# Weighted sums of attention in four groups a step in place of nine

## What is computed

```python
x = L0_attn_x                       # (4, 1024, 256)
xn = _layernorm(x)
x = x + attention(xn) + experts(xn)
# attention: 16 heads of 16 features, scores q k^T, causal mask, a linear bias
#   slope[h] * (j - i), divided by 4, softmax, weighted sum of v, then @ Wo + bo
# experts: 8 experts of 256 hidden features, each token goes to 2 of them;
#   gelu(a) * b, a second product, scaled, summed by the router's weights
```

## Time and profile before

| what | us |
|---|---|
| median of 3 runs | 816.59 (814.65 to 817.5) |
| the profiled execution | 818.57 |
| its span, first to last instruction | 816.8 |
| attention, t = 0 to 4 | 132.82 |
| attention, t = 5 to 12 | 219.84 |
| attention, t = 13 | 25.96 |
| attention, t = 14 and 15 | 47.5 |

### The profile page before, as it was taken

How to read it: one execution, slowest core, us unless ns; L and a number is a source line. 1 busy time by engine, 2 the same in 40 slices (tenths; PEclk the granted TensorE clock), 3 DMA queues, 4 the chain that set the end, 5 groups by cost and what they waited for, 6 DMA issues and landing times.

```text
span 816.8 us, 17685 instructions
## 1 busy us (share of the span) xinstructions
PE 768.0 (94%) x6172; PEld 470.9 (58%) x6172; DVE 545.4 (67%) x1419; ACT 467.1 (57%) x984; POOL 429.9 (53%) x561
## 2 busy tenths in 40 slices
PE   7899999999999999999999999879899999989997
PEld 5555554444444444444444444329788888888876
DVE  5458879999999887888888888303234434334348
ACT  2565557777778677777777777874233323323310
POOL 5765542231324545645475463255586666666676
PEclk9999999999999999999999999999899999999999
DMA  8786562503233135243342350113533333322777
GB/s 199 229 253 218 170 193 74 157 17 106 82 93 85 52 95 132 51 109 100 110 98 71 94 159 16 37 40 97 139 106 108 112 116 102 111 78 87 234 237 243
DMA packets 74912, 98.20 MB, mean 120 GB/s; under 512 B 16588, under 2 KB 54092, under 8 KB 74764
## 3 DMA queue, kind: packets, MB, share of 16 engines
q1 hardware_dynamic: 65960, 78.34, 34.1%
q0 software_dynamic: 8864, 18.72, 7.4%
HBM read 63.53 MB, written 30.75 MB: 115 GB/s over the span
## 4 chain that ended last, share of the span: by engine, by line
PE 55%; issue 10%; POOL 8%; ACT 4%; DVE 4%; DMA 2%; another core or an unknown queue 1%; DVEq 0%; POOLq 0%; ACTq 0%
PE banks L1152 16%; PE banks L753 15%; PE banks L745 13%; PE banks L1337 7%; POOL expert_rows L1241 4%; ACT probs L1090 4%; PE banks L1346 3%; POOL stacks L592 3%; DVE stacks L1436 2%; DMA stacks<-xn_rows,places 2%; PE banks L1267 1%; DVE junk L707 1%; DMA w_gu<-expert_rows 0%; DVE probs L1319 0%
## 5 line engine op out<-in xcount | busy, mean ns | idle before, releaser
L707 DVE CUSTOM_DVE_ANT_0 junk<-banks,mask 128x128 bf16<-128x128 f32 (+7 forms) x512 | 359.3, 752 | 54.9 <-issue 50.8
L1090 ACT ACTIVATE probs<-banks 128x512 f32<-128x512 f32 x576 | 310.9, 607 | 101.2 <-PE banks L753 93.7
L753 PE MATMUL banks<-stacks 105*128 105x512 bf16 (+3 forms) x768 | 198.8, 328 | 10.5 <-issue 7.8
L745 PE MATMUL banks<-stacks 102*128 102x512 bf16 (+3 forms) x768 | 172.6, 326 | 2.7 <-DVE maxima L707 2.4
L883 POOL TENSOR_SCALAR_AFFINE_SELECT probs<-probs 128x512 f32<-128x512 f32 x128 | 79.6, 640 | 102.3 <-ACT probs L1090 98.3
L1319 DVE TENSOR_TENSOR probs<-banks,probs 128x256 f32<-128x256 f32 x71 | 30.0, 422 | 151.5 <-ACT probs L1283 111.9
L753 PEld LDWEIGHTS banks<-stacks 105*128 105x128 bf16 x768 | 65.5, 97 | 103.5 <-ACT probs L1090 38.0
L1152 PE MATMUL banks<-probs,ctxT 128*17 128x256 f32 (+2 forms) x1920 | 114.4, 360 | 2.0 <-DVE banks L1071 1.1
L1241 POOL DMA_INDIRECT expert_rows<-stacks,places x71 | 77.5, 1091 | 67.9 <-ACT stacks L1288 51.7
L745 PEld LDWEIGHTS banks<-stacks 102*128 102x128 bf16 x768 | 69.0, 98 | 73.1 <-DVE maxima L707 18.5
L1283 ACT ACTIVATE probs<-banks 128x256 f32<-128x256 f32 x71 | 27.3, 384 | 111.9 <-PE banks L1337 56.4
(11 more groups left out here) (129 smaller groups left out, 769.6 us busy)
## 6 DMA issues: line engine op xcount, KB each, us to landing
stacks<-qk_parts SPq DMA_DIRECT2D x192, 128.0 KB, 3.1
qk_parts<-ctxT SPq DMA_DIRECT2D x32, 384.0 KB, 3.4
xn_rows<-probs SPq DMA_DIRECT2D x8, 512.0 KB, 5.3
ctxT<-inverse_sums SPq DMA_DIRECT2D x8, 512.0 KB
w_gu<-in_w_gu SPq DMA_DIRECT2D x8, 512.0 KB
stacks<-in_x SPq DMA_DIRECT2D x16, 256.0 KB
ctxT<-expert_rows SPq DMA_DIRECT2D x16, 256.0 KB, 3.1
w_gu<-expert_rows SPq DMA_DIRECT2D x16, 256.0 KB, 5.8
```

The source lines that it names most:

```text
L707: last = dve.tensor_tensor_reduce(junk[:, n % RING, c:c + w], mpsum[:, slot, c:c + w], keep["mask"][:, S - w:S], 1.0, 3 * NEG, ALU.add, AL ...
L745: last = pe.matmul(mpsum[:, slot, at + c:at + e], qs[hq][0:R_MAX, h, qt * P:(qt + 1) * P], ks[hq][0:R_MAX, h, c:e], start=True, stop=True)
L753: last = pe.matmul(score_bank(("S", n, h))[:, c:c + w], ks[hq][:, h, kt * P:(kt + 1) * P], qs[hq][:, h, q0:q0 + w], start=True, stop=True)
L1090: act.activation(probs[:, u % PRING, h], score_bank(("S", n, h)), ACT.Exp, scale=SCALE).then_inc(exp_done, 1)
```

## The change

The weighted sums of steps 0 to 13 are issued in four groups: after p = 4 (5 halves), 9 (5), 13 (4) and 17 (4). So a buffer of probabilities is held longer, and there are four of them in steps 0 to 13; the fourth lies in the last quarter of `w_gu`, so the weights of experts 6 and 7 are loaded in steps 14 and 15 and no longer in steps 11 and 12. Steps 14 and 15 keep the order and the three buffers of before. ACT waits for the last user of its buffer (`PROB_WAS`). Count and sizes of the matmuls, exponentials, maxima and DMAs stay.

```diff
-PRING = 3
+PRING = 4
+PROBS = 3
 SRING = 3
+FEW_FROM = B * NQ - 2
+
+def prob_buffers():
+    buffer, was, last = [], [], {}
+    for n in range(B * NQ * NU):
+        k = n - NU * FEW_FROM
+        buffer.append(n % PRING if k < 0 else (k + 2) % PROBS)
+        was.append(last.get(buffer[n]))
+        last[buffer[n]] = n
+    return buffer, was
+
+PROB_BUF, PROB_WAS = prob_buffers()
...
 PV_AT[4], PV_AT[5], PV_AT[7] = [LOW_LAST], [], [HIGH_FIRST, (3, 0), (3, 1)]
+PV_GROUPED = [[] for _ in range(PAIRS)]
+PV_GROUPED[4] = [(0, 0), (0, 1), (1, 0), (1, 1), LOW_LAST]
+PV_GROUPED[9] = [HIGH_FIRST, (3, 0), (3, 1), (4, 0), (4, 1)]
+PV_GROUPED[13] = [(5, 0), (5, 1), (6, 0), (6, 1)]
+PV_GROUPED[17] = [(7, 0), (7, 1), (8, 0), (8, 1)]
...
-    qs, ks, vals, probs = heads["qs"], heads["ks"], keep["vals"], keep["probs"]
+    qs, ks, vals = heads["qs"], heads["ks"], keep["vals"]
+    probs = [keep["probs"][:, i] for i in range(PROBS)] + [Room(keep["w_gu"][:, 3 * NE * DH // 4:].rearrange("p e h -> p (e h)"))([P, 4, CH])]
...
-            if MAP_FROM <= t < MAP_FROM + NE:
-                e = t - MAP_FROM
+            if t >= FEW_FROM:
+                sp.wait_ge(pv_done, PRING + NU * FEW_FROM)
+            for e in [t - MAP_FROM] if MAP_FROM <= t < MAP_FROM + 3 * NE // 4 else [NE - B * NQ + t] if t >= FEW_FROM else []:
                 sp.dma_start(keep["w_gu"][:, e * DH:(e + 1) * DH], ...
...
-            if h == 0:
-                act.wait_ge(pv_done, n + 1)
-            act.activation(probs[:, u % PRING, h], ...
+            if h == 0 and PROB_WAS[n] is not None:
+                act.wait_ge(pv_done, PRING + PROB_WAS[n] + 1)
+            act.activation(probs[PROB_BUF[n]][:, h], ...
...
-                for u0, half in PV_AT[p] if has(1) else PV_LAST[p]:
+                for u0, half in (PV_GROUPED if t < FEW_FROM else PV_AT if has(1) else PV_LAST)[p]:
...
-        keep["probs"] = sb("probs", [P, PRING, 4, CH])
+        keep["probs"] = sb("probs", [P, PROBS, 4, CH])
```

More of the change, by code:

```diff
@@ L881, in mask_unit @@
             for c in DIAG[u]:
-                part = probs[:, u % PRING, :, c:c + P]
+                part = probs[PROB_BUF[n]][:, :, c:c + P]
                 pool.affine_select(out=part, in_=part, compare_op=ALU.is_ge, fill=0.0, base=0,
@@ L1087, in exp @@
             act.wait_ge(s_ready, m + 1)
-            if h == 0:
-                act.wait_ge(pv_done, n + 1)
-            act.activation(probs[:, u % PRING, h], score_bank(("S", n, h)), ACT.Exp, scale=SCALE).then_inc(exp_done, 1)
+            if h == 0 and PROB_WAS[n] is not None:
+                act.wait_ge(pv_done, PRING + PROB_WAS[n] + 1)
+            act.activation(probs[PROB_BUF[n]][:, h], score_bank(("S", n, h)), ACT.Exp, scale=SCALE).then_inc(exp_done, 1)
         for h in range(4):
@@ L1151, in weighted @@
                 for h in range(4):
-                    last = pe.matmul(cpsum[32 * h:32 * h + VW, q0 % CH:q0 % CH + w], vals[b][:, kt, hq, h], probs[:, u % PRING, h, c:c + w],
+                    last = pe.matmul(cpsum[32 * h:32 * h + VW, q0 % CH:q0 % CH + w], vals[b][:, kt, hq, h], probs[PROB_BUF[n]][:, h, c:c + w],
                                      start=i == 0 and (u, half) in ((0, 0), HIGH_FIRST),
```

## The result

| what | before | after |
|---|---|---|
| median of the runs, us | 817.05 (814.65 to 822.0) | 838.68 (837.11 to 840.26) |
| the profiled execution, us | 818.57 | 838.23 |
| its span | 816.8 | 836.5 |
| attention, t = 0 to 4 | 132.82 | 144.41 |
| attention, t = 5 to 12 | 219.84 | 228.33 |

The four groups make the kernel slower: ratio 1.0263, 95% interval 1.0238 to 1.0288, 21.6 us. All of it lies in the attention. What follows the attention takes 266.6 us, as before (266.7).

A forecast was written before the change was run, and what follows sets the result against it. PE was taken as first by a small margin, with DVE setting the pace after the change; +1.6, +17.1, +4.2 and +5.6 make +28.5 on 818.57, so 847.1 profiled and 845 us median, range 824 to 860.

The forecast's parts named there:

- t = 13, DVE dry in four gaps: Step 13: DVE's work plus four idle gaps make 27.6 us against 25.96, +1.6.
- t = 5 to 12, gaps, router's rest and indirect DMAs: Steps 5 to 12: +4.2 us for gaps and other DVE operations, +5.6 for sums meeting POOL's DMAs (0.7 a step).
- t = 0 to 4, gaps and router: Steps 0 to 4: gaps, plus 11.9 us of router operations outside them, make 149.9 us against 132.82, +17.1.
- t = 14 and 15: Last two attention steps: no term in the sum; moved weight loads expected to be hidden.
- PE's saving: PE, steps 0 to 13: five groups fewer at 0.25 us each save 1.25 us a step, 17.5 if PE alone sets pace.
- waits for slots: PE between groups: the third and later product items wait for DVE to free a slot, giving back the 1.25 us.
- DVE's idle, 0.42k - 0.50: DVE behind each group of k halves: idle 1.21 us for k = 4 and 1.63 for k = 5.
- first by a small margin: Kernel before: PE leads, DVE at most two product items behind; both busy 98% in steps 0 to 4.
- PE sets the pace: Rival, steps 0 to 13: DVE's slots never hold PE, 17.5 us are saved, 799 us; chance 0.08.
- Edits at no cost: Fourth buffer, ACT's waits and later w_gu loads cost nothing; moving loads gains PE and DVE 0 to 0.5 us.
- ACT idle on the sums: Sign at L1152 that the edit fails, ACT waiting for its buffer; that rival: 873 us, chance 0.03.
- ACT catches up before the next group: ACT, needing 20.38 of 25.96 us, idles in a group with three banks but recovers before the next; no cost.

The follow-up runs named there:

- e6: Changed kernel (four groups) with half of the columns of both maxima and exponentials left out; ratio 0.9719 to the kernel before.
- e2: Kernel before (nine groups) with half of the columns of every maximum left out; ratio 0.9871 to the kernel before.
- e3: Changed kernel (four groups) with half of the columns of every maximum left out; ratio 0.9853 to the kernel before.
- e5: Changed kernel with full maxima, but exponentials over half of their columns from the fifth unit on; ratio 1.0277 to the kernel before.
- e7: Changed kernel with seven groups of two or three halves in place of four, fourth buffer kept; ratio 1.0102 to the kernel before.
- e8: Changed kernel with the router's DVE operations put behind the maxima of pairs that end in a group; ratio 1.0285 to the kernel before.
- e11: e1 with one indirect DMA behind each of units 2 to 9, not two behind each of 6 to 9; ratio 0.9897 to the kernel before.
- e1: Changed kernel with the sums back in nine places, fourth buffer and later w_gu loads kept; ratio 0.9971 to the kernel before.
- e12: e6 with one indirect DMA behind each of units 2 to 9 of steps 5 to 12; ratio 0.9664 to the kernel before.
- e9: Kernel before with POOL's indirect DMAs behind units 2 to 5 instead of 6 to 9; ratio 1.0684 to the kernel before.

## Why the prediction was right, point by point

The forecast was 845 us and 28.5 us of loss on the profiled execution; it came to 838.7 and 19.7.

| term | forecast | measured |
|---|---|---|
| t = 13, DVE dry in four gaps | +1.6 | +1.7 |
| t = 5 to 12, gaps, router's rest and indirect DMAs | +9.8 | +8.5 |
| t = 0 to 4, gaps and router | +17.1 | +11.6 |
| t = 14 and 15 | 0 | -2.0 |

- **PE's saving.** 0.25 us a group from the earlier trace rows; e6 against e2 gives 0.27 at most and about 0.16 without the waits for ACT. So that PE gains by fewer groups is shown, its exact price is not. In the changed kernel it is given back in waits for slots, as forecast.
- **DVE's idle, 0.42k - 0.50.** Forecast 1.21 and 1.63, found 1.23, 1.23, 1.66, 1.77. Step 13: 27.6 forecast, 27.62 found. So close a meeting is luck, for cut at DVE's items instead of ACT's copy the same step is 28.01 (26.35 before); the difference of 1.66 us is the same by both cuts. e3 and e5 show that it is DVE: take its work away and the step falls by 1.3 us, take ACT's away and it doesn't fall. The text called PE "first by a small margin" in the kernel before; e2 confirms PE. That DVE's work and idle time, 22.17 and 3.79, add up to the step proves nothing, since they do so whoever sets the pace. What shows how small the margin was is e7: two groups fewer already cost 0.8 us in step 13. From this point on DVE pays more for a merging than PE gains.
- **The rival "PE sets the pace", 799 us.** In the changed kernel it is false. In e6, with both consumers light, PE does set the pace and the saving is real. The Trainium skill, "TensorEngine Tiling (Array Packing)", section Key Properties, says that TensorE drains when the tiling mode changes. The 0.25 us a group of the earlier trace rows agree with it; but the sums differ from the scores in their type too, and no run separates the two. What the saving is worth depends on who must be fed.
- **Steps 0 to 4, the term that was mis-sized.** I let two thirds of 17.8 us of router operations lie outside the gaps, because only three groups end an odd pair. But five steps at 27.62 are 138.1, and the stretch took 144.41: 6.3 us lay outside, a good third. In step 4 the gaps left DVE idle for less than in step 13:

```profile
247.83 1.23 DVE L731 CUSTOM_DVE_ANT_0 junk<-banks,mask 128x1024 bf16<-128x1024 f32 x1 [1.32 <-issue]
...
256.24 1.23 DVE L731 CUSTOM_DVE_ANT_0 junk<-banks,mask 128x1024 bf16<-128x1024 f32 x1 [0.73 <-PE banks L769]
262.36 1.23 DVE L731 CUSTOM_DVE_ANT_0 junk<-banks,mask 128x1024 bf16<-128x1024 f32 x1 [0.30 <-issue]
```

  Gaps of 1.32 in place of 1.66 (p = 4, an even pair), 0.73 in place of 1.77 and 0.30 in place of 1.23. My reading is that an operation in the pair ahead of the group's also helps, because it keeps the last items in the slots until PE is in the group; no run tests that alone. e8's 3.3 us in four steps agree with a rest of that size.
- **Steps 5 to 12.** I took 0.7 us a step for sums that meet the indirect DMAs. These steps take 28.24 at their most frequent, 0.6 over step 13, and 28.5 on average. The size was about right; that this cost was in the kernel before too, larger (1.2 a step), and could be removed, e11 showed.
- **Edits at no cost.** DVE's first copy of experts' weights waited 17.3 us in step 15 and nobody was late for it: the stage behind takes the same time. ACT idle on the sums did not occur. That ACT catches up before the next group holds in the changed kernel (e5) and no longer with a light DVE (e3). But steps 14 and 15 gained 2.0 us, 1.9 of it also in e1. For step 15 the rows show how: in the kernel before PE stood still for 2.30 us behind sums that met POOL's six gathers, afterwards for 0.81. The first two rows are of before (POOL's last gather, PE), the third of after:

```profile
542.29 0.95 POOL L592 DMA_INDIRECT stacks<-xn_rows,places  x1 [0.30 <-issue]
...
544.39 0.39 PE L753 MATMUL banks<-stacks 105*128 105x384 bf16 x2 [2.30 <-issue]
```

```profile
565.52 1.09 PE L1177 MATMUL banks<-probs,last_vals 128*17 128x384 f32 x16 [0.81 <-issue]
```

  The gathers stand elsewhere against the sums now; that is luck. Step 14 gained 0.9 with DVE's first copies of experts' weights no longer in it. In the kernel before they ran from 518.56 on the earlier trace rows, while POOL split the maxima of step 15, and two of POOL's operations took 0.69 and 0.72 us where they take 0.25 and 0.29 in the changed kernel; PE waited 1.25 us for the split, afterwards 0.38. The second of them before and after:

```profile
519.44 0.72 POOL L695 TENSOR_SCALAR msplit<-mrest 128x32 bf16<-128x32 f32 x1
```

```profile
540.75 0.29 POOL L719 TENSOR_SCALAR msplit<-mrest 128x32 bf16<-128x32 f32 x1
```

  So the moved loads, which I had put at no gain for DVE and PE (0 to 0.5 us), gave nearly half of the 2.0 us by keeping DVE's copies away from the split.

What stays open besides: by what mechanism a group of sums is held while GpSimd issues indirect DMAs, and whether float32, the column tiles or the operand's place matter; no run varied them.

## What to carry to other kernels

A producer that serves two consumers through two slots and three banks must not be away longer than these hold. Add up for each consumer its work and the idle time that the new gaps will bring, worked out from the length of the absence and from what the slots hold, as for DVE here (21.9 and four gaps of 0.42k - 0.50, 27.6 in all). When that is more than the step of today, a saving on the producer that lengthens its absences is a loss, however busy the producer looks. Before moving such work, look for waits that come from elsewhere: single DMAs in place of two in a row gained 1.0% here, and no regrouping of the sums at full work gained anything.

## What the hardware showed that I had not expected

- **Matmuls behind sums that meet GpSimd's indirect DMAs are delivered late**, and the longer GpSimd's run of DMAs, the later: under the resolution of a step with single DMAs (e11), 1.1 us a step with pairs in the kernel before, 1.6 in e12, where one pair is left, some 7 us with eight in a row (e9). PE's records show nothing of it. The Trainium skill, "Perfetto Trace Analysis", section "Per-instruction lifecycle: what the profiler-reported window actually captures", says that TensorE's end times are computed and that the semaphore goes out only when PSUM has the data; the trace agrees, with records that end at 375.1 and a consumer that starts at 381.88. The Trainium skill, "SBUF — State Buffer", section "Who interferes with whom", says that PE never waits on anyone; it speaks of ports, and whether this is one isn't known, but in e9 PE's results come only behind GpSimd's last DMA (379.96), and the measurement decides.
- **During or behind such a stand the clock can fall.** In e9 PE stands still for 6.11 us, from 376.4 to 382.5. TensorE is granted 1.00 before, 0.77 on average from 377 to 380, its lower level (1.2 of 2.4 GHz) from 380 to nearly 389, when PE has long been at work again, and 1.00 from then on:

```profile
377.00:380.00 3.00, 0.00 (x0) 0.00 (x0) 0.00 (x0) 0.00 (x0) 2.35 (x3) 0.77 0.10 25
380.00:389.00 9.00, 6.47 (x34) 2.05 (x38) 4.91 (x12) 4.20 (x8) 1.36 (x5) 0.51 0.01 1
```

  In e11's step 5 the lower level sets in during the wait of 5.3 us, and 0.79 is granted over the 11.5 us behind it; in e8 it is 0.54 over 7.2 us behind a stand of 1.41 us. So a stand of PE can cost more than its own length. It need not: behind the 2.30 us of step 15 in the kernel before the granted clock stayed at 1.00.
- **Two of GpSimd's small operations took 0.69 and 0.72 us beside DVE's copies of 128x1024, and 0.25 and 0.29 without them** (step 14, before and after; in e2 and e9, where the copies meet them too, 0.68 and 0.72).
